# Between two layers: the second norm by batch, batch 1's split on GpSimd, the first maxima ahead of the gate rows

## The reference: two layers of attention times a gated expert network

```python
xn = _layernorm(x, axis=-1)
s = _L1_attn_ref(xn, ...)     # 16 heads of 8 channels, causal softmax(Q K^T / sqrt(8)) V, then W_O
g = _silu(_L1_ffn_ref(xn, ...))
x = x + s * g

def _L1_ffn_ref(x, ...):
    n1 = _layernorm(x, ln1_w, ln1_b)          # a second norm, of the normalised tokens
    rw = _gating(n1, smha_sim, smha_gates)    # logits = n1/|n1| @ sim/|sim| - sigmoid(gates)
    # expert attention with rw on q, k, v and the output, then
    # a second norm and gate, and eight gelu experts
```

## Time and profile before

| | |
|---|---|
| median of 3 runs | 1200.33 us (1199.22 to 1203.84) |
| profiled execution | 1205.69 us, span 1203.9 us |
| TensorE busy in the span | 1068.8 us (89%) |
| VectorE, ScalarE, GpSimd busy | 814.8, 646.0, 201.9 us |
| mean granted TensorE clock | 0.938 |
| the first layer's attention ends, the second's half 0 starts | about 600, 679.43 us |

### The profile page before, as it was taken

One profiled execution on the slowest core, in us unless ns is written; L12 is line 12 of the kernel. 1 busy time (PEld: TensorE's weight loads), 2 busy tenths in 40 slices (PEclk: granted clock), 3 DMA queues, 4 the chain that ended last, 5 costly groups with the idle time before them and its releaser, 6 DMA issues.

```text
span 1203.9 us, 19384 instructions
## 1 busy us (share of the span) xinstructions
PE 1068.8 (89%) x7308; PEld 496.2 (41%) x7308; DVE 814.8 (68%) x1621; ACT 646.0 (54%) x1258; POOL 201.9 (17%) x323
## 2 busy tenths in 40 slices
PE   5799999999999999999864799889989999988767
PEld 4455555552222222222233343334444478444444
DVE  6656666667887888883377587888872255565654
ACT  4522222217898888989622256667775533432534
POOL 2244554510010101011000001123320000000000
PEclk9799999999999999999976688999997999998888
DMA  4674121000110110000034013211322020000431
GB/s 117 206 227 140 49 79 66 1 10 19 30 42 29 43 32 27 18 13 21 10 122 142 28 39 80 76 48 50 129 97 80 11 79 1 1 1 0 142 141 35
DMA packets 57398, 74.63 MB, mean 62 GB/s; under 512 B 15720, under 2 KB 35032, under 8 KB 55512
## 3 DMA queue, kind: packets, MB, share of 16 engines
q1 hardware_dynamic: 48516, 62.13, 16.2%
q10 hardware_dynamic: 8788, 11.26, 3.2%
HBM read 58.18 MB, written 14.54 MB: 60 GB/s over the span
## 4 chain that ended last, share of the span: by engine, by line
PE 70%; DVE 18%; ACT 7%; issue 3%; DMA 1%; ACTq 0%; SPq 0%; POOL 0%; DVEq 0%
PE PS L1806 68%; DVE mx L1575 9%; ACT arena L1074 5%; PE PS L1819 1%; DVE arena L1374 1%; DVE arena L1780 1%; PE PS L2278 0%; DVE arena L1377 0%; DVE arena L1338 0%; DVE arena L1326 0%; DVE small L1766 0%; DMA arena<-mrow 0%; DMA arena<-in_L_attn_x 0%; ACT arena L1027 0%; DVE fw L1671 0%
## 5 line engine op out<-in xcount | busy, mean ns | idle before, releaser
L1806 PE MATMUL PS<-arena 128*32 128x512 f32 (+12 forms) x3656 | 565.8, 474 | 60.9 <-DVE mx L1575 23.4
L1575 DVE TENSOR_REDUCE mx<-PS 128x1 f32<-128x512 f32 (+3 forms) x896 | 512.3, 623 | 82.8 <-PE PS L1806 78.6
L1074 ACT ACTIVATE arena<-PS 128x512 f32<-128x512 f32 (+3 forms) x896 | 435.4, 559 | 149.7 <-PE PS L1806 145.7
L1806 PEld LDWEIGHTS PS<-arena 128*32 128x32 f32 (+3 forms) x3656 | 147.1, 104 | 416.9 <-ACT arena L1074 183.8
L1806 PE MATMUL PS<-x_hi,w_hi_lo 128*128 128x512 f32 x320 | 145.5, 496 | 7.0 <-POOL x_lo L991 2.6
L1117 ACT ACTIVATE fw<-PS 128x512 f32<-128x512 f32 x80 | 47.8, 597 | 168.1 <-PE PS L1806 168.1
L1671 DVE TENSOR_TENSOR fw<-PS,fw 128x512 f32<-128x512 f32 x80 | 55.3, 692 | 79.1 <-PE PS L1806 75.1
L1806 PE MATMUL PS<-fw 128*128 128x512 f32 (+3 forms) x184 | 99.2, 625 | 0.0
L985 POOL TENSOR_TENSOR fw<-fw,arena 128x512 f32<-128x512 f32 x64 | 81.8, 1280 | 75.7 <-DVE fw L1671 75.7
L917 POOL TENSOR_TENSOR arena<-arena,fw 128x512 f32<-128x512 f32 x31 | 39.8, 1284 | 296.6 <-DMA fw<-sum_dram 296.6
L1806 PEld LDWEIGHTS PS<-x_hi,w_hi_lo 128*128 128x128 f32 x320 | 61.2, 191 | 38.4 <-issue 21.5
(11 more groups left out here) (315 smaller groups left out, 1113.9 us busy)
## 6 DMA issues: line engine op xcount, KB each, us to landing
arena<-comb_dram SPq DMA_DIRECT2D x14, 1024.0 KB, 4.9
arena<-comb_dram SPq DMA_DIRECT2D x18, 512.0 KB, 7.3
fw<-sum_dram SPq DMA_DIRECT2D x31, 256.0 KB
q_dram<-arena SPq DMA_DIRECT2D x24, 256.0 KB, 4.0
k_dram<-arena SPq DMA_DIRECT2D x24, 256.0 KB, 4.2
arena<-k_dram ACTq DMA_DIRECT2D x20, 204.0 KB
arena<-q_dram ACTq DMA_DIRECT2D x20, 192.0 KB
arena<-drev_dram SPq DMA_DIRECT2D x16, 192.0 KB, 6.8
```

Source lines behind the costliest of these rows:

```text
L1074: s.activation(Pr[:, m % 8, 0:w], st_bank(l, m, 0, w), ACT.Exp).then_inc(A["e_done"], 1)
L1575: v.reduce_max(mx[:, H % 2, kh, n:n + 1], bank(ring_bank[l][U], 0, w), axis=AX.X, negate=True).then_inc(A["ring_free"], 1)
L1806: return nc.tensor.matmul(out_, lhsT, rhs, start=start, stop=stop)
```

## The change

1. **Second norm by batch.** `layer_norm(4, ztok, zz)` goes. `batch_norm` takes the statistics of its eight scaled tiles right behind the scaling (`moments`), ahead of the copy of the transposed tokens, and `normal_again` scales them to `zz`: for batch 0 behind `normalised(0)`, for batch 1 behind `queries(1)`. ScalarE takes one root per batch and norm.
2. **Batch 1's split on GpSimd.** `split_rest(1, 1)` goes from VectorE. GpSimd does its four subtractions, two ahead of the first maxima's parts and two behind them. SyncE's stores of batch 1 wait for them and stand behind `max_rows(1, 0)`.
3. **Batch 1's products in other banks.** Queries in banks 6 and 7, keys in 4 and 5, instead of 0 to 3, so the score units wait only for batch 0's values; the transposes of `zz` take the wait for keys and values.
4. **First maxima ahead of the gate rows.** K and M of half 0 stand right behind its 16 units. TensorE does the transposes of `zz`, then M and the other 14 units, and the gate rows last; VectorE copies the logits behind all first units.
5. **Counts.** Half 0's steps take 8, 8, 8 and 10 units. The eight others move the rest of the list: units run out in the last step of half 13.

```diff
@@ s_stream
+        if layer == 1 and H == 0:
+            stream += [("K", H), ("M", H)]
+            continue
         late += [("K", H, COMBINE_AFTER), ("M", H, MAX_AFTER[layer])]
@@ even_steps
-            count = HG if H else (10, 10, 10, 12)[i]
+            count = HG if H else (8, 8, 8, 10)[i]
@@ buffers
-        q32b, k32b = [at(16, 4), at(80, 4)], [at(20, 4), at(84, 4)]
+        q32b, k32b = [at(16, 4), at(24, 4)], [at(20, 4), at(28, 4)]
+        late_pairs = ((q32b[1], qspb[1]), (k32b[1], kspb[1]))
@@ SyncE, attention_feed
-                for H in range(LAG[l]):
-                    max_rows(l, H)
...
+                max_rows(l, 0)
+                store_qk(sp, 1, 1)
+                max_rows(l, 1)
@@ SyncE, behind the loads of groups 0 and 1
-            store_qk(sp, 1, 1)
@@ GpSimd, attention
-                pool.wait_ge(v_ev, 4 * (l + 1))
+                pool.wait_ge(v_ev, 4 if l == 0 else 6)
...
-                for H in range(LAG[l]):
-                    max_parts(H)
+                for n, (src, dst) in enumerate(late_pairs):
+                    pool.wait_ge(hi_done, 4 + 2 + n + 1)
+                    g.tensor_tensor(src, src, dst[:, 0, :], ALU.subtract).then_inc(rest_done, 1)
+                max_parts(0)
+                for n, (src, dst) in enumerate(late_pairs):
+                    pool.wait_ge(mid_done, 4 + 2 + n + 1)
+                    g.tensor_tensor(dst[:, 2, :], src, dst[:, 1, :], ALU.subtract).then_inc(rest_done, 1)
+                max_parts(1)
@@ ScalarE, between the layers
                 if b:
-                    batch_root(1)
+                    batch_root(1, 4)
+                batch_root(b, 3 + 2 * b)
...
-            root_var(4)
@@ VectorE
-            def batch_norm(b, st):
+            def moments(b, st, src):
                 part = slice(KT * b, KT * (b + 1))
...
+                for t in range(KT * b, KT * (b + 1)):
+                    ins = v.bn_stats(st[:, t - KT * b, :], src[:, t, :])
...
+            def scaled(b, n, src, dst):
+                part = slice(KT * b, KT * (b + 1))
+                dve.wait_ge(rstd_ready, n)
+                own.link(v.reciprocal(small[:, 2, part], small[:, 2, part]))
...
+            def batch_norm(b, st):
+                for c in (2 * b, 2 * b + 1):
+                    dve.wait_ge(tr_ps, 8 + 4 * b + c % 2 + 1)
+                    v.tensor_copy(xtok[:, 4 * c:4 * c + 4, :].rearrange("p t c -> p (t c)"), bank(row_bank(c))).then_inc(tr_ev, 1)
+                dve.wait_ge(tr_ev, 8 + 4 * b + 2)
+                moments(b, st, xtok)
+                scaled(b, 2 + 2 * b, xtok, ztok)
+                dve.wait_ge(z_ready, 4 * b + 6)
+                moments(b, st, ztok)
+
+            def normal_again(b):
+                scaled(b, 3 + 2 * b, ztok, zz)
@@ VectorE, between the layers
             normalised(0)
+            normal_again(0)
...
             queries(1)
-            split_rest(1, 1)
+            normal_again(1)
             batch_values(1)
-            layer_norm(4, ztok, zz)
@@ VectorE, attention
-                    sequence(first_units[l][:AHEAD])
+                    sequence(first_units[l])
                     gate_raw(1)
-                    sequence(first_units[l][AHEAD:])
@@ TensorE, attention
                     for what in first_units[l][:AHEAD]:
                         ring_unit(what)
-                    transposes(lambda t: zz[:, t, :], 4, lambda c: pe.wait_ge(z_ready, 8 + c + 1))
+                    pe.wait_ge(k_ev, 8)
+                    pe.wait_ge(v_ev, 8)
+                    transposes(lambda t: zz[:, t, :], 4, lambda c: pe.wait_ge(z_ready, (7, 8, 11, 12)[c]))
+                    for what in first_units[l][AHEAD:]:
+                        ring_unit(what)
                     pe.wait_ge(tr_ev, 20)
                     gate_rows(1, n1T, 4, 6)
                     pe.wait_ge(ss_ready, 1)
-                    for what in first_units[l][AHEAD:]:
-                        ring_unit(what)
@@ TensorE, between the layers
-                for w, first, done in ((wq, (4, 0)[b], q_ps), (wk, (6, 2)[b], k_ps)):
+                for w, first, done in ((wq, (4, 6)[b], q_ps), (wk, (6, 4)[b], k_ps)):
...
+            pe.wait_ge(k_ev, 6)
+            queries_keys(1)
+            pe.wait_ge(q_ev, 8)
+            token_values(1)
             pe.wait_ge(v_ev, 6)
-            queries_keys(1)
-            pe.wait_ge(k_ev, 6)
-            token_values(1)
-            pe.wait_ge(q_ev, 8)
-            pe.wait_ge(k_ev, 8)
-            pe.wait_ge(v_ev, 8)
             attention(1)
```

More of the change, by code:

```diff
@@ L603, in store_qk @@
         def store_qk(eng, l, b):
-            eng.wait_ge(split_done, 4 * l + 2 * b + 1)
+            if l == 1 and b == 1:
+                eng.wait_ge(rest_done, 9)
+            else:
+                eng.wait_ge(split_done, 4 * l + 2 * b + 1)
             for part, row, times in Q_ROWS:
@@ L611, in store_qk @@
                     eng.dma_start(dst, src).then_inc(qk_stored[l][b], 16)
-            eng.wait_ge(split_done, 4 * l + 2 * b + 2)
+            if l == 1 and b == 1:
+                eng.wait_ge(rest_done, 10)
+            else:
+                eng.wait_ge(split_done, 4 * l + 2 * b + 2)
             for row, parts in K_ROWS:
@@ L699, in attention_feed @@
                 A = att[l]
-                for H in range(LAG[l]):
-                    max_rows(l, H)
-                    if H == 0:
-                        then.get(-1, nothing)()
+                max_rows(l, 0)
+                store_qk(sp, 1, 1)
+                max_rows(l, 1)
                 for H in range(HALVES):
@@ L1067, in attention @@
                         if l == 0 and H == HALVES - 1 and i == 6:
-                            batch_root(0)
+                            batch_root(0, 2)
                         if n >= 2:
@@ L1244, in chain @@
                 if n == plan["sqrt"]:
-                    act.wait_ge(var_ready, 5 + b)
+                    act.wait_ge(var_ready, 6 + b)
                     part = slice(KT * b, KT * (b + 1))
@@ L1340, in layer_norm @@
                         ins.then_inc(z_ready, 1)
-            def batch_norm(b, st):
+            def moments(b, st, src):
                 part = slice(KT * b, KT * (b + 1))
-                m_, v_, r_, d_ = small[:, 0, part], small[:, 1, part], small[:, 2, part], small[:, 3, part]
-                for c in (2 * b, 2 * b + 1):
-                    dve.wait_ge(tr_ps, 8 + 4 * b + c % 2 + 1)
-                    v.tensor_copy(xtok[:, 4 * c:4 * c + 4, :].rearrange("p t c -> p (t c)"), bank(row_bank(c))).then_inc(tr_ev, 1)
-                    dve.wait_ge(tr_ev, 8 + 4 * b + c % 2 + 1)
-                    for t in range(4 * c, 4 * c + 4):
-                        ins = v.bn_stats(st[:, t - KT * b, :], xtok[:, t, :])
+                m_, v_, d_ = small[:, 0, part], small[:, 1, part], small[:, 3, part]
+                for t in range(KT * b, KT * (b + 1)):
+                    ins = v.bn_stats(st[:, t - KT * b, :], src[:, t, :])
                 own.link(ins)
@@ L1360, in batch_norm @@
                 v.tensor_scalar(v_, v_, LN_EPS, None, ALU.add).then_inc(var_ready, 1)
-                dve.wait_ge(rstd_ready, 2 + b)
-                own.link(v.reciprocal(r_, r_))
+            def scaled(b, n, src, dst):
+                part = slice(KT * b, KT * (b + 1))
+                dve.wait_ge(rstd_ready, n)
+                own.link(v.reciprocal(small[:, 2, part], small[:, 2, part]))
                 for t in range(KT * b, KT * (b + 1)):
-                    ins = v.tensor_scalar(ztok[:, t, :], xtok[:, t, :], small[:, 0, t:t + 1], small[:, 2, t:t + 1], ALU.subtract, ALU.mult)
+                    ins = v.tensor_scalar(dst[:, t, :], src[:, t, :], small[:, 0, t:t + 1], small[:, 2, t:t + 1], ALU.subtract, ALU.mult)
                     if t % 4 == 3:
                         ins.then_inc(z_ready, 1)
+            def batch_norm(b, st):
[9 more added lines that the diff above has]
+                scaled(b, 3 + 2 * b, ztok, zz)
             def split_rest(l, b):
@@ L1516, in second_norm @@
                 part = slice(KT * b, KT * (b + 1))
-                dve.wait_ge(rstd_ready, 5 + b)
+                dve.wait_ge(rstd_ready, 6 + b)
                 own.link(v.reciprocal(small[:, 2, part], small[:, 2, part]))
@@ L2212, in _ @@
             pe.wait_ge(q_ev, 6)
-            transposes(lambda t: ztok[:, t, :], 2, lambda c: pe.wait_ge(z_ready, 4 + c + 1), (2, 3))
+            transposes(lambda t: ztok[:, t, :], 2, lambda c: pe.wait_ge(z_ready, 6 + c + 1), (2, 3))
             pe.wait_ge(tr_ev, 16)
+            pe.wait_ge(k_ev, 6)
+            queries_keys(1)
+            pe.wait_ge(q_ev, 8)
+            token_values(1)
             pe.wait_ge(v_ev, 6)
-            queries_keys(1)
-            pe.wait_ge(k_ev, 6)
-            token_values(1)
-            pe.wait_ge(q_ev, 8)
-            pe.wait_ge(k_ev, 8)
-            pe.wait_ge(v_ev, 8)
             attention(1)
```

10 lines of the change are left out of this document (6 added, 4 removed).

## The result

The changed kernel takes 1195.56 us in the median of nine runs (1190.6 to 1197.21), the kernel before beside it 1202.0 (1199.06 to 1204.33). The ratio is 0.9942, with 95% interval 0.9924 to 0.996: faster by 6.4 us, where 14.8 were forecast. The profiled execution took 1190.6 us (span 1188.8).

What follows compares the result with a forecast made beforehand. TensorE was taken as the bound, with a hole from 640 to 680 us where it waits, mainly for VectorE. Terms -16.7 - 3.0 + 1.4 + 1.0 + 2.5 = -14.8 us gave 1185.5 us, range 1178 to 1196.

Steps and rivals of the forecast that it cites:

- Half 0: First 512 queries of the first four heads, second attention: starts at 662.7 instead of 679.43, 16.7 us earlier, behind the logits' copies.
- the price of the norm by batch: Batch 1's products start at 632.9 instead of 628.56, because scalings and 3.0 us of statistics stand ahead.
- The load of the operands, taken as in time: First score units start at 641.0 without waiting for their operands' DMA; if it landed late, 644, 3 us worse.
- GpSimd: Batch 1's subtractions take 2.6 us each, at most 5.1, and slow VectorE's maxima by 0.
- Rival 3: GpSimd is the bound: 5.1 us a subtraction, maxima blocked beside it, 2 + 10 us of gain gone, 1197.5; chance 0.05.
- Shorter half 0 (-3.0): Half 0's four steps carry 34 score units instead of 42, saving 3.0 us where VectorE is the bound.
- The late rows of odd halves (+1.0): Maxima of odd halves 3 to 13 finish two steps later, so their row DMAs may land late: 0.2 us a half.
- Rival 1: Odd halves' rows land 9.6 us after their copy, six halves 3.2 late: 1203.7; chance 0.05 in full, 0.08 milder.
- Half 13 (+1.4): The eight units taken from half 0 return in half 13's last two steps, costing 1.4 us.
- The sums (+2.5): Sums' DMA queues behind row DMAs; VectorE waits in halves 10 and 12, charged 2.5 us, between 0 and 6.
- Rival 2: The slow clock lasts through all of halves 0 and 1, costing 5.5 us: 1191; chance 0.12.
- rival 4: Better than forecast: waits for sums and rows covered (3.5), clock rises at once (2.4): 1179.6; chance 0.08.

Runs made afterwards that it cites:

- experiment 7: Changed kernel with the old counts 10, 10, 10, 12 and one second norm over all 16 tiles behind the value copies: 1189.53 us, ratio 0.9893 to the kernel before.
- experiment 6: Changed kernel with the old counts 10, 10, 10, 12 and batch 1's four subtractions back on VectorE: 1190.95 us, ratio 0.9911 to the kernel before.
- experiment 2: Changed kernel with only half 0's counts put back to 10, 10, 10 and 12 units: 1182.17 us, ratio 0.9866 to the kernel before.
- experiment 10: Changed kernel with half 0's counts 8, 8, 8, 10 kept, but the eight other units put into half 1: 1183.77 us, ratio 0.9859 to the kernel before.
- experiment 1: Changed kernel with SyncE loading the gate rows of halves 9 to 13 behind the sums' DMA: 1185.49 us, ratio 0.9881 to the kernel before.
- experiment 3: Changed kernel with SyncE's queue ordered sums, maxima's rows, gate rows, then inverted sums: 1187.52 us, ratio 0.9898 to the kernel before.
- Experiment 4: Kernel before with only half 0's counts changed to 8, 8, 8 and 10: 1211.76 us, ratio 1.0115 to the kernel before.
- experiment 11: Changed kernel with old counts, sums ahead of rows on SyncE, ScalarE's group 2 loads ahead of its copies, run again: 1183.72 us, ratio 0.9862 to the kernel before.
- experiment 9: Changed kernel with old counts and batch 1's queries and keys back in banks 0 to 3: 1183.35 us, ratio 0.987 to the kernel before.

## Why the prediction was right in direction and wrong in size

- **Half 0, right.** Forecast: earlier by 16.7, released by the logits. Measured: 19.2, released by them. The points on the way were near: products 631.61 (632.9), first maxima 639.39 (641.9), their copy 649.01 (651.5). The products came 1.3 earlier than forecast: the first layer ended 0.2 earlier, batch 0's scalings cost 0.9 and not 1.3 on the path, and batch 1's statistics 2.4 and not 3.0, because two short waits of VectorE for the transposes (0.25 and 0.27) fell away. In experiment 7 they start 3.5 us earlier than in its base, so the price of the norm by batch is real; taking it out costs 6.2 net.
- **The load of the operands, taken as in time: right**, and so was the reason given. In the kernel before SyncE issued the next group's load at 637.15, so the first group's had landed by then; the idle time up to 642.65 in the earlier trace rows was the value copies, which ended at 642.40. In the changed kernel the load had landed by 637.84, 0.8 us ahead of the first unit (638.67).
- **GpSimd, right.** 4.21 us a pair, 2.1 each, where 2.6 was taken and 5.1 was the upper bound. The 16 maxima beside it took the same 6.65 us as without it in the earlier trace rows, and experiment 6 says the same of the other 14. Rival 3 is false.
- **Shorter half 0 (-3.0).** From its start to its reciprocal 33.9 us against 36.1: 2.2 saved. But against experiment 2, which has the old counts and all else alike, it is 0.8 (34.7), and experiment 10, with the same light half 0, gains nothing in the whole. The forecast says that the first step's eight units hide ScalarE's table load; they did not, TensorE idled for 1.98 us behind it, 0.82 in experiment 2.
- **The late rows of odd halves (+1.0): nothing.** TensorE waited for rows once, 0.6 us. Rival 1 needed 3.2 in each of six halves; it is false.
- **Half 13 (+1.4).** From the reciprocal of half 12 to that of half 15 it takes 62.48 us against 63.65, with a clock of 0.92 against 0.89. No cost is seen, and none could be told from the clock's own play.
- **The sums (+2.5): the step that failed.** The place, the halves and the cause were named as they came out: VectorE late by 3 to 4 us in half 10 and perhaps 2 in half 12 (4.71 and 2.16; the wait of over 4 us named as a sign came in half 10 alone). What was wrong is what they cost: "TensorE can run four units, 2.2 us, ahead in the ring, so I charge 2.5 for both, between 0 and 6". The ring covered next to nothing: in half 10 TensorE stood for 4.19 of VectorE's 4.71 us. And the clock fell behind it, which the forecast had no term for. The term measures 11.1 us in the trace, 10.6 in experiment 1's (68.3 against 78.85), and lies outside its bounds. Against experiment 3, which has the same order of units and no such wait (12.42, 15.68, 12.23, 15.68 and 12.23 us), the three stretches that hold the waits are 7.26 us longer and the two behind them 3.35. Experiment 4 gives the sum of all that the counts do: +12.6, where the forecast's terms make -3.0 + 1.4 + 1.0 + 2.5 = +1.9.
- **Halves 1 to 7: no term at all.** The lead fell from 21.5 to 20.0 us there, and against experiment 2 the changed kernel loses 4.6 (114.6 against 110.0). One place is the stretch from the reciprocal of half 1 to that of half 2: it takes 14.54 us at a granted clock of 0.88, against 13.07 at 1.00; TensorE idles 1.39 us for ScalarE in it, 0.79 in experiment 2. That the one causes the other is not shown: the kernel before idles 0.80 there and has 0.88 too.
- **The sum again with what was measured**: -19.2 (half 0 earlier) - 2.2 (its length) + 1.5 (halves 1 to 7) + 11.1 (halves 8 to 12) - 1.2 (halves 13 to 15) = -10.0, the lead at the last reciprocal. The medians say 6.4 (interval 4.8 to 9.1). The remaining 3.6 are not settled: the traces are of one execution each, and the code behind the last reciprocal alone, the same in all, takes 238.8 us in the changed kernel's trace, 243.9 in the one before and 243.9 in experiment 11's. The measured 1195.56 us still lies in the stated range of 1178 to 1196, by 0.4 us; that is luck: half 0 came 2.5 us better than forecast and the sums 8.6 worse.
- **Rival 2, the slow clock**: in 680 to 700 it is 0.85 where it was 0.70, so it did not last longer there. The rival had the right kind of loss in the wrong place. Its price was misread: the maxima of 0.42 and of 0.54 us in the earlier trace rows were both taken at a clock of 0.50, and differ because 11 of the 17 later ones are 512 wide and only 4 of the first 16. A maximum over 512 takes 0.68 us at a clock of 0.50 and of 1.00. The same misreading stands behind the 2.4 of rival 4.

Undoing one item moves half 0 back by 9.5, 8.6, 6.2 and 2.4 us (items 4, 2, 1, 3). These make 26.7, more than the 18.2 that they bring together. The likely reason is that several waits stood one behind the other, and each item undone lets one of them end last again; no pair of items was undone to test it.

## What to carry to other kernels

A small transfer that an engine waits for must not be queued behind large ones: its place in the issuing queue decides more than the traffic beside it. Where one step in a list is made shorter, look at what slides behind it; put the taken work into the next step and the rest keeps its place. Price an idle time of TensorE in a full stretch at more than its length where the traces show the clock falling behind such times: here 4.19 us of it cost 2.2 more. And where a row names a transfer as what ended a wait, look when the transfer that was needed had landed: in experiment 9 it was another one.

## What the runs showed of the hardware

- Gate rows (1 MB each, two of them) ahead of the 8 KB of sums on one queue made them land 5.4 us after their issue (836.33 to 841.78), one gate row 4.2 (869.88 to 874.11); with no gate row ahead 1.9 (819.93 to 821.86, half 9), and with the two gate rows right behind them at most 2.4 (839.53 to 841.96 in experiment 1). The Trainium skill, page "DMA: Bandwidth & Descriptors" (Two DMAs through the same engine are not ordered), says that within a queue of a DMA engine descriptors start in order; these numbers agree with it.
- After 4.19 us of idle TensorE the mean granted clock of the stretch behind was 0.71 (14.40 us, where experiment 3 with the same order of units took 12.23 at 1.00); after the 1.64 us of half 12 it was 0.87 (13.41 against 12.23), with 0.50 from 878 to 880, where TensorE is busy throughout.
- VectorE's maxima do not go by TensorE's clock. In the kernel before one over 512 elements took 0.678 us in the mean where the granted clock was 0.50 (11 of them from 680.32 on), and 0.675 where it was 1.00 (24 of them, 828.64 to 857.13); one over 128 took 0.28 us in both.
- A GpSimd subtraction of 128x1024 took 2.1 us where its product of 128x512 takes 1.28, less than twice.
